# Output stage: inverse roots for two tiles at a time, scatters issued ahead of the root, one step less from root to scaling

## The reference

```python
x = _layernorm(x + _L0_gnn_ref(x, edge_index, L0_gnn_W, ...))          # attention over edges, 4 heads of 64
x = _layernorm(x + _L1_gnn_ref(x, edge_attr_64, edge_index, ...))      # attention over edges, 4 heads of 32
# inside the second layer, for each node:
out  = segment_sum((v[src] + e) * alpha, dst)                          # 128 wide
beta = sigmoid(concat([out, x_r, out - x_r]) @ Wbeta.T)                # x_r: skip branch
y    = (beta * x_r + (1 - beta) * out) @ W_m2n.T
# _layernorm(z) = (z - mean(z)) / sqrt(var(z) + 1e-5)
```

## Time and profile before

| | |
|---|---|
| Time of the kernel, median of 3 runs | 1322.01 us (1320.61 to 1337.71) |
| The profiled execution's own time | 1323.17 us |
| Its span, first to last instruction | 1321.3 us |
| Busy, share of the span: PE / DVE / ACT / POOL | 90% / 79% / 63% / 63% |
| Granted TensorE clock, mean | 0.971 |
| HBM | 159.67 MB read, 117.12 MB written |

### The profile page before, as it was taken

How to read it: one execution, slowest core, us unless ns; L and a number is a source line. 1 busy time by engine, 2 the same in 40 slices (tenths; PEclk the granted TensorE clock), 3 DMA queues, 4 the chain that set the end, 5 groups by cost and what they waited for, 6 DMA issues and landing times.

```text
span 1321.3 us, 28295 instructions
## 1 busy us (share of the span) xinstructions
PE 1187.7 (90%) x6982; PEld 1022.6 (77%) x6982; DVE 1041.0 (79%) x3766; ACT 837.5 (63%) x2783; POOL 838.6 (63%) x1046
## 2 busy tenths in 40 slices
PE   3799999999997799999999799999999967988883
PEld 3688998989995688888887699998899946766662
DVE  3467677777769799999998799999999967776663
ACT  0366566666667766666667565665665685877775
POOL 4688888888863445555555667776766541565556
PEclk9899999999998899999999899999999987999997
DMA  6658888888873578788785777777777523544441
GB/s 178 201 191 274 265 270 269 262 268 268 265 228 124 175 242 260 252 263 260 247 255 179 248 225 219 221 216 213 220 216 219 156 102 117 163 153 147 146 142 67
DMA packets 208795, 276.99 MB, mean 210 GB/s; under 512 B 40045, under 2 KB 140420, under 8 KB 208634
## 3 DMA queue, kind: packets, MB, share of 16 engines
q1 hardware_dynamic: 188793, 224.13, 53.7%
q0 software_dynamic: 19264, 50.85, 12.7%
q10 hardware_dynamic: 576, 0.20, 0.1%
HBM read 159.67 MB, written 117.12 MB: 209 GB/s over the span
## 4 chain that ended last, share of the span: by engine, by line
PE 69%; DVE 16%; issue 6%; ACT 3%; another core or an unknown queue 3%; DMA 1%; POOL 1%; DVEq 0%; SPq 0%; ACTq 0%; POOLq 0%
PE banks L744 20%; PE banks L857 7%; PE banks L734 6%; PE banks L1385 5%; PE banks L1587 5%; PE banks L847 3%; PE banks L1220 3%; DVE AT L1246 3%; PE banks L1372 3%; PE banks L859 2%; PE banks L1390 2%; PE banks L1595 2%; PE banks L1213 2%; PE banks L1591 2%
## 5 line engine op out<-in xcount | busy, mean ns | idle before, releaser
L744 PE MATMUL banks<-m_ext,node_XT 128*128 128x257 f32 x1568 | 379.6, 385 | 0.0
L744 PEld LDWEIGHTS banks<-m_ext,node_XT 128*128 128x128 f32 x1568 | 286.7, 193 | 33.8
L770 DVE SCALAR_TENSOR_TENSOR node_X<-banks,node_be,node_X 128x256 f32<-128x256 f32 x392 | 169.4, 474 | 83.9 <-ACT node_be L696 61.9
L671 POOL TENSOR_TENSOR node_r<-node_vv,half 128x4 f32<-128x4 f32 (+1 forms) x202 | 215.2, 1065 | 17.2 <-POOL node_vv L666 0.3
L702 ACT ACTIVATE node_XT<-banks 128x512 f32<-128x512 f32 x196 | 117.5, 599 | 130.8 <-PE banks L734 122.7
L666 POOL TENSOR_SCALAR node_vv<-node_mv 128x4 f32<-128x4 f32 (+1 forms) x202 | 58.2, 288 | 193.7 <-DVE node_mv L778 174.0
L709 ACT ACTIVATE node_sq<-node_X 128x256 f32<-128x256 f32 x392 | 157.8, 408 | 0.0
L683 ACT ACTIVATE node_X<-node_X,node_r 128x256 f32<-128x256 f32 x326 | 146.0, 497 | 1.4 <-POOL node_r L671 1.4
L763 DVE BATCH_NORM_STATS2 node_st<-node_X 128x6 f32<-128x256 f32 x392 | 145.3, 412 | 1.3 <-issue 0.5
L734 PE MATMUL banks<-ident,node_X 128*128 128x128 f32 x784 | 122.3, 279 | 18.2 <-issue 9.6
L824 POOL DMA_INDIRECT ring<-in_x,src_col x100 | 106.5, 1065 | 34.4 <-issue 14.5
(11 more groups left out here) (265 smaller groups left out, 2712.9 us busy)
## 6 DMA issues: line engine op xcount, KB each, us to landing
node_X<-in_x SPq DMA_DIRECT2D x196, 256.0 KB
out<-node_X SPq DMA_DIRECT2D x196, 256.0 KB
ring<-rows SPq DMA_DIRECT2D x210, 128.0 KB
rows<-ring SPq DMA_DIRECT2D x100, 256.0 KB
rows<-ring SPq DMA_DIRECT2D x200, 128.0 KB
MB<-keeps SPq DMA_DIRECT2D x40, 320.0 KB, 4.6
store<-rows SPq DMA_DIRECT2D x90, 128.0 KB
MB<-picks SPq DMA_DIRECT2D x50, 128.0 KB
```

The lines of the kernel that those rows point to most:

```text
L671: pool.tensor_tensor(r[:, s % 4, NT * lo:NT * hi], v, self.c.half[:, NT * lo:NT * hi], ALU.pow).then_inc(self.roots, 1)
L744: last = pe.matmul(ps[:, NT * o + k, 0:D + 1], self.XT[:, o, k * D + h * P:k * D + (h + 1) * P], c.m_ext[:, h, :], start=(h == 0), stop=(h ...
L770: last = dve.scalar_tensor_tensor(out=X[:, n % U, k, :], in0=ps[:, b + k, 0:D], scalar=self.be[:, n % 4, k:k + 1], in1=X[:, n % U, k, :], ...
```

## The change

Three edits in Output. The groups become 1, 1, forty-eight times 2, and 1, 1, so there are 52. The scaling stands at `_last + 7 + k` in place of `_last + 8 + k`, the scatter still one step after it. In a step POOL's scatters stand ahead of its roots. With tiles in pairs, the last tile of a pair is odd: at an odd step POOL has one scatter and then one root, at an even step one scatter. The buffers of variances and roots (`max(GROUPS)` wide) get narrower with the groups.

```diff
-GROUPS = (1, 2, 3, 4) + (G,) * 16 + (4, 3, 2, 1)
+GROUPS = (1, 1) + (2,) * 48 + (1, 1)
 ...
     for _k in range(_size):
-        _at = max(_last + 8 + _k, _at)
+        _at = max(_last + 7 + _k, _at)
         SCALED_AT.setdefault(_at, []).append(GROUP_AT[_g] + _k)
         SCATTERED_AT.setdefault(_at + 1, []).append(GROUP_AT[_g] + _k)
 ...
         def emit(t):
-            for g in ROOTS_AT.get(t, ()):
-                size = GROUPS[g]
-                pool.wait_ge(self.widened, g + 1)
-                at_least(pool, self.y_ready, GROUP_AT[max(0, g - 2)])
-                pool.tensor_tensor(self.r[:, g % 3, 0:size], self.va[:, g % 3, 0:size], c.half_row[:, 0:size], ALU.pow).then_inc(self.roots, 1)
             for n in SCATTERED_AT.get(t, ()):
                 ...
                 pool.wait_ge(self.y_ready, n + 1)
                 pool.indirect_dma_start(out=self.out, ...).then_inc(self.scattered, 16)
+            for g in ROOTS_AT.get(t, ()):
+                size = GROUPS[g]
+                pool.wait_ge(self.widened, g + 1)
+                at_least(pool, self.y_ready, GROUP_AT[max(0, g - 2)])
+                pool.tensor_tensor(self.r[:, g % 3, 0:size], self.va[:, g % 3, 0:size], c.half_row[:, 0:size], ALU.pow).then_inc(self.roots, 1)
```

## The result

The changed kernel takes **1282.46 us** (median of 4 runs, 1281.43 to 1287.04); in the same rounds the kernel before took 1321.31 us (4 runs, 1320.18 to 1337.71). The ratio of the runs is **0.971, 95% interval 0.9692 to 0.9727**. Forecast were 1284 us and a range of 1279 to 1314.

What follows compares the result with a forecast made beforehand. TensorE sets the 1.64 us step in Output, but its updates become known late while POOL issues a third or later scatter without rest. 32.5 (steps) plus 6.4 (end) is 38.9 us saved: 1323.2 - 38.9 = 1284 us, range 1279 to 1314.

Steps and rivals of the forecast that it cites:

- Groups and root times: Output on POOL: 52 roots, 0.74 us for two tiles, 0.59 for one; a pair costs POOL 3.26 us, TensorE 3.28.
- Holds: TensorE's updates, 0.94 us late beside a third scatter, are not held by pairs of scatters with 0.94 us between pairs.
- 87 steps: Steady part of Output: 1.66 us a step, 144.4 us (142.7 to 147.9) in place of 177.0, 32.5 us saved.
- One mark: Sign that the holds are gone in Output: no wait of a scan above 0.5 us.
- Rival 2: Half of the holds stay in Output: 1.87 us a step, 162.7 us for 87 steps, 1302 us; chance 0.17.
- rival 3: Holds belong to scatters in whatever order, 0.46 us each: 2.10 us a step, 1322 us; chance 0.12.
- rival 4: Slower: every scatter holds TensorE's updates by 0.94 us, 2.58 us a step, 1364 us; chance 0.05.
- Scatters ahead of the root: POOL's order in a step: root ends 1.36 us after the scan, 0.28 us before ACT's scaling of the next step.
- the sign that POOL is the bound: ACT's scaling waiting for roots step after step would make POOL the bound and the forecast wrong.
- One step less: Scaling one step nearer its root: nothing in the steady part of Output, a shorter end.
- The end: From the last scan to the end of the span: 17.1 us in place of 23.47, 6.4 us saved.
- rival 1: DVE's message product (L1648) waits for POOL's roots: 0.42 us a pair, 18.5 us, 1303 us; chance 0.04.

Runs made afterwards that it cites:

- Pairs alone: Kernel before with groups of two tiles only; old order in a step and old distance from root to scaling stay: 1286.70 us, ratio 0.974.
- the rests put into fives: Kernel before, groups of five, with an added POOL power instruction behind the second and fourth scatter of each row of five: 1305.15 us, ratio 0.980.
- threes: Changed kernel with groups of three tiles in place of two: 1293.72 us, ratio 0.977.
- fours at the end: Changed kernel with the last eight tiles in two groups of four in place of 2, 2, 2, 1, 1: 1283.53 us, ratio 0.967.
- pairs and order without the step less: Changed kernel with the old distance from root to scaling (`_last + 8 + _k`): 1282.17 us, ratio 0.962.
- fours and the old distance up to the last tiles: Changed kernel with its last eight tiles in two fours, and the old root-to-scaling distance ahead of the last twelve tiles: 1283.79 us, ratio 0.968.
- the kernel without roots: Changed kernel with the inverse roots left out, rows scaled by the widened variance, POOL having only scatters: 1288.55 us, ratio 0.966.

## Why the prediction was right, point by point

**Groups and root times.** 48 roots of two and 4 of one were forecast at 0.74 and 0.59 us; the 44 in the steady part have a mean of 0.751. POOL's round was put at 3.26 and takes 3.26 to 3.32, TensorE's at 3.28. POOL is as close to the bound as forecast; from 1120 to 1250 us it waits for no other engine that the trace can name, and TensorE is busy for 129.0 of the 130 us.

**Holds.** That a pair and a rest of 0.94 us hold nothing was the choice on which the sum stood. Pairs alone gave 161.7 us for 98 steps, 1.65 each; the rests put into fives took 23.9 us out of the steps, and the third scatter of threes brought a late scan back. These three show the row of scatters without a rest as the cause. It isn't their rate: the changed kernel makes ten steps, a scatter in each, in 16.4 us, the kernel before in 21.0. Nor is it the masks that SP loads every five tiles, which are the same in all of these kernels. That it is TensorE's update that comes late, and not TensorE, is read from its transposes in the kernel before, which answer to the scans of 1188.12, 1190.51 and 1194.13 in the earlier trace rows:

```profile
1187.81 0.27 PE L1591 MATMUL banks<-ident,MSG 128*128 128x128 f32 x1
...
1189.45 0.27 PE L1591 MATMUL banks<-ident,MSG 128*128 128x128 f32 x1
...
1191.14 0.30 PE L1591 MATMUL banks<-ident,MSG 128*128 128x128 f32 x1
```

They end 0.04, 0.79 and 2.69 us ahead of their scans.

87 steps were put at 144.4 us; from scan 12 to scan 99 the changed kernel takes 144.0:

```profile
1117.44 0.48 DVE L1663 TENSOR_TENSOR_SCAN S<-MB,S,banks 128x128 f32<-128x128 f32 x1
...
1194.56 0.48 DVE L1663 TENSOR_TENSOR_SCAN S<-MB,S,banks 128x128 f32<-128x128 f32 x1 [0.57 <-PE banks L1591]
1195.92 0.47 DVE L1663 TENSOR_TENSOR_SCAN S<-MB,S,banks 128x128 f32<-128x128 f32 x1
...
1261.48 0.48 DVE L1663 TENSOR_TENSOR_SCAN S<-MB,S,banks 128x128 f32<-128x128 f32 x1 [0.26 <-PE banks L1591]
```

The saving is 32.9 us where 32.5 were forecast. One mark was missed slightly: from scan 12 on the longest wait of a scan is 0.6 us and not under 0.5. So a pair isn't wholly free: nine scans of the changed kernel start 0.3 to 0.55 us after their transpose has ended, none in pairs alone or without the step less. Such waits are caught up, as the scans of 1194.56 (0.57 late) and 1195.92 show, 1.36 apart. Ten steps, from the scan of 1181.06 to that of 1197.46, take 16.40 us, where 16.5 were forecast. That the sum met 144.0 so closely is in part luck: the 0.02 us a step allowed for small waits (1.7 us in all) came as 1.5 us, of which 1.0 is one wait that the sum had put at nothing (below). Rival 2 (half of the holds, 162.7 us) falls with the 144.0; rival 3 (holds belong to scatters in any order) falls with the rests in fives, which keep every scatter; rival 4 (slower) with all of them.

**Scatters ahead of the root.** Here a step of the prediction failed. It put the root's end 0.28 us ahead of ACT's scaling, since the scatter ahead of it would be over by the time of the widening. In the trace the widening is done at 1183.18, POOL is on a scatter until 1184.31, and the scaling of 1181.78 waited 0.31 us for its root; such waits come to 14.4 us in the 88 steps. With POOL all but full its work runs late, and a time taken from a trace in which POOL rested 2.93 us a group doesn't carry over. The prediction had named these waits as the sign that POOL is the bound. They weren't: from 1120 to 1250 us TensorE waits once, for 1.00 us. POOL had paused for 1.74 us ahead of the scatter of 1136.03, for a reason that the trace doesn't show; the root behind came late, ACT's scaling waited for it, ACT's copy (L1610) stands behind the scaling, and TensorE waits for the copy:

```profile
1139.15 0.51 ACT L1628 ACTIVATE store<-store,output_r 128x256 f32<-128x256 f32 x1 [1.85 <-POOL output_r L1544]
...
1140.13 0.41 PE L1577 MATMUL banks<-ident,store 128*128 128x128 f32 x2 [1.00 <-ACT AT L1610]
```

The prediction had seen that the next step's copies queue behind the scaling; it had the time to spare wrong.

**One step less.** Forecast as nothing in the steady part and as part of the shorter end. The first half failed, by little. The 87 steps take 144.0, 144.0 and 143.9 us in the three profiled runs with the step less throughout (the changed kernel, the same again, fours at the end), each with that one wait of TensorE of 1.0 us. They take 142.5 us with the old distance, in pairs alone and in pairs and order without the step less, where POOL has a pause of 1.9 and 2.2 us too and TensorE waits for nothing. With fours and the old distance up to the last tiles they take 143.3, with one wait of 0.7 us where the new distance sets in. So the step less costs some 1.5 us in the steps and gives 2.3 back at the end; the medians (1282.46 and 1281.93 with it, 1282.17 without) don't show the difference.

**The end.** 17.1 us were forecast, 18.1 came. The 1.77 us behind the last scatter are as put: it starts at 1276.86, takes 0.97 and the span ends at 1279.60. What failed is where POOL stands: ten scatters start after the last scan and not nine, and the root of tiles 92 and 93 starts 1.62 us after that scan and not 0.62, since the first of the ten is ahead of it. That is the same step as above, and just the 1.0 us. POOL's timeline, the first scatter of the ten, that root, and the last scatter:

```profile
1262.11 0.98 POOL L1538 DMA_INDIRECT out<-store,last_col  x1 [0.30 <-issue]
1263.10 0.75 POOL L1544 TENSOR_TENSOR output_r<-output_va,half_row 128x2 f32<-128x2 f32 x1
...
1276.86 0.97 POOL L1538 DMA_INDIRECT out<-store,last_col  x1 [0.30 <-issue]
```

**Message products beside roots.** They take 0.286 us in the mean of 86 with the added roots, and 0.282 in the kernel before, none with a wait ahead of it. In the changed kernel they hardly meet the roots, so it tests rival 1 little: only two of 99 lie wholly inside a root, 0.28 us each. The test is the kernel before, where 20 lie wholly inside a root and each takes 0.28, as the one of 1185.83 does. Rival 1, DVE held by the roots, has nothing for it. That is the rule of the Trainium skill (SBUF — State Buffer, section "SBUF: two separate sides") by which the two would lock each other out; these 20 disagree with it.

The sum of 38.9 us stands against 38.3 in the two stretches (32.9 and 5.4), and the rest of the 41.7 was no part of the change.

## What to carry to other kernels

When an engine waits for another that has long been done, look at what a third one issues at that moment; here the late updates of TensorE went with rows of three and more indirect transfers on POOL, and a pause of 0.66 us behind each, or of 0.94 behind every second one, took all but small remains of them away. Spread indirect transfers over the steps rather than saving small instructions between them: work put in between them can pay for itself. And on an engine that a change makes nearly full, take start times from its own queue, not from the trace in which it still rested.

## What was not expected of the hardware

- More work on POOL made the kernel faster: 32 added instructions of 0.75 us, 98 steps 23.9 us shorter in the profiled run.
- Rows keep themselves going. Without roots one late scatter made a row of five, its hold bunched the next four, and only then was the even spacing of one scatter per step back; later the same came about once more.
- A gap of 0.66 us between indirect transfers leaves TensorE's updates on time, rows of three and more with gaps of 0.30 to 0.53 don't.
- Rows of three plain stores on the same engine, 0.55 us each, hold nothing.

What stays open: why an indirect transfer on POOL keeps TensorE's updates back, whether it is its issue or its packets, the indirect form or the time that a row keeps POOL, and whether gathers do the same; none of these was tried. What delayed the scatter of 1146.16 in the kernel without roots is not known either; POOL pauses for 1.7 to 2.2 us at about the same place in pairs, where no row follows.
